# Value products on array quarters, a two-piece mask, transposed statistics, half of the query norms inside the exponential, and re-ordered queues

## The reference

```python
qkv = x @ Wqkv;  q, k, v = split(qkv)                  # 128 -> 3 * 1024
q = l2norm(q) * qs;  k = l2norm(k) * ksc               # norm over each head's 64 numbers
q = q * cos * scale + rotate_half(q) * sin * scale     # and k with 1 / scale
sim = q . k * 8 (own window and the one before);  masked;  attn = softmax(sim);  out = attn @ v
x = x + out @ Wo
xn = (x - mean) / sqrt(var + 1e-5) * g + b
x = x + (a * gelu(gate)) @ W2,   a, gate = split(xn @ W1 + b1)
```

## Time and profile before

| what | value |
|---|---|
| median of 3 runs | 3455.47 us (3453.51 to 3456.21) |
| the profiled execution's own time | 3455.64 us |
| its span, first to last instruction | 3453.9 us |
| PE busy (matmul) | 3233.1 us, 94% |
| DVE busy | 3171.4 us, 92% |
| POOL busy | 2706.3 us, 78% |
| ACT busy | 2438.2 us, 71% |
| mean granted clock of PE | 0.978 of full |

### The profile page before, as it was taken

How to read it: one execution, slowest core, us unless ns; L and a number is a source line. 1 busy time by engine, 2 the same in 40 slices (tenths; PEclk the granted TensorE clock), 3 DMA queues, 4 the chain that set the end, 5 groups by cost and what they waited for, 6 DMA issues and landing times.

```text
span 3453.9 us, 108159 instructions
## 1 busy us (share of the span) xinstructions
PE 3233.1 (94%) x45916; PEld 2089.8 (61%) x46108; DVE 3171.4 (92%) x2914; ACT 2438.2 (71%) x3945; POOL 2706.3 (78%) x1265
## 2 busy tenths in 40 slices
PE   5657999999999999999999999999999999999996
PEld 3325666666666666666666666666666666666663
DVE  6759999999999999999999999999999999999992
ACT  4645777777777777777777777777777777777764
POOL 4547888888888888888878888888888888888871
PEclk9889999999999999999999999999999999999996
DMA  2001111122111122111122111112211122211111
GB/s 77 2 0 32 40 42 39 40 55 57 38 44 39 39 53 57 41 42 42 38 52 54 47 39 41 42 51 52 50 39 40 42 52 51 49 41 39 41 41 39
DMA packets 150433, 148.32 MB, mean 43 GB/s; under 512 B 39228, under 2 KB 95424, under 8 KB 149952
## 3 DMA queue, kind: packets, MB, share of 16 engines
q1 hardware_dynamic: 149952, 141.39, 16.6%
HBM read 19.62 MB, written 2.10 MB: 6 GB/s over the span
## 4 chain that ended last, share of the span: by engine, by line
PE 38%; DVE 26%; ACT 12%; issue 10%; POOL 5%; SPq 2%; DMA 1%; ACTq 0%; DVEq 0%; POOLq 0%
PE bank L574 11%; PE bank L673 7%; DVE rot L1405 6%; PE mid L583 4%; DVE rot L1411 4%; DVE raw L1397 4%; PE mid L624 4%; PE bank L644 4%; DVE Pr L1369 4%; PE mid L611 4%; ACT sq L911 3%; POOL FX L1164 3%; ACT mid L944 3%; DVE mx L1347 2%; ACT raw L903 2%
## 5 line engine op out<-in xcount | busy, mean ns | idle before, releaser
L574 PE MATMUL bank<-wqkv,xs 128*128 128x512 f32 x2304 | 1133.0, 605 | 11.0 <-ACT raw L903 8.5
L1145 POOL TENSOR_TENSOR rr<-ssm,nhalf 128x32 f32<-128x32 f32 x192 | 1051.8, 5478 | 16.0
L1155 POOL TENSOR_TENSOR swp<-raw,TS 128x1024 f32<-128x1024 f32 x384 | 896.8, 2356 | 175.1 <-DVE raw L1397 175.1
L903 ACT ACTIVATE raw<-bank 128x512 f32<-128x512 f32 x768 | 447.5, 598 | 424.2 <-PE bank L574 258.4
L574 PEld LDWEIGHTS bank<-wqkv,xs 128*128 128x128 f32 x2304 | 394.4, 191 | 310.4 <-issue 267.2
L1397 DVE TENSOR_TENSOR raw<-raw,rr 128x2048 f32<-128x2048 f32 x192 | 489.9, 2552 | 16.8 <-POOL rr L1145 16.8
L1391 DVE TENSOR_REDUCE ss<-sq 128x16 f32<-128x1024 f32 x384 | 463.5, 1207 | 23.7 <-ACT sq L911 12.1
L583 PE MATMUL mid<-ident,rot 128*128 128x128 f32 x3072 | 416.6, 279 | 52.0 <-DVE rot L1411 23.1
L583 PEld LDWEIGHTS mid<-ident,rot 128*128 128x128 f32 x3072 | 336.9, 142 | 204.1 <-ACT OT L950 134.6
L1411 DVE TENSOR_TENSOR rot<-rot,swp 128x2048 f32<-128x2048 f32 x192 | 440.1, 2292 | 21.1 <-DVE rot L1405 1.4
L1405 DVE TENSOR_TENSOR rot<-raw,TC 128x2048 f32<-128x2048 f32 x192 | 434.1, 2261 | 0.0
(11 more groups left out here) (134 smaller groups left out, 4443.8 us busy)
## 6 DMA issues: line engine op xcount, KB each, us to landing
PT<-PTd SPq DMA_DIRECT2D x1344, 64.0 KB
xs<-F SPq DMA_DIRECT2D x192, 64.0 KB, 1.9
wqkv<-d_wqkv SPq DMA_DIRECT2D x36, 256.0 KB, 3.3
VT<-V SPq DMA_DIRECT2D x144, 64.0 KB
BT<-PTd SPq DMA_DIRECT2D x288, 32.0 KB
fwo<-d_fwo SPq DMA_DIRECT2D x6, 512.0 KB, 4.1
d_out<-X SPq DMA_DIRECT2D x8, 256.0 KB, 2.3
w<-d_w SPq DMA_DIRECT2D x6, 341.0 KB
```

The costliest lines, as they stand in the source:

```text
L574: nc.tensor.matmul(bank[bk][:, :], xs[:, j, :], wqkv[:, c, :], start=True, stop=True)\
L903: nc.scalar.activation(raw[:, j % 2, c * 512:(c + 1) * 512], bank[RAW_BANK[c]][:, :], ACT.Copy)\
L1145: pool.tensor_tensor(rr[:, :], ssm[:, :], nhalf[:, :], ALU.pow).then_inc(rr_ready, 1)
L1155: last = pool.tensor_tensor(dst[:, :, :, t, :], src[:, :, :, 1 - t, :], tab.unsqueeze(2).broadcast_to([P, 2, HEADS, 32]), ALU.mult)
```

## The change

- **Value products.** `pv` becomes `pv_first` and `pv_second`. Each head's product of 128 keys by 128 queries is cut into one of the lower 64 keys by 96 queries and one of the upper 64 keys by 64 queries, on quarters of the array; the products with the keys in front come first and now use 64 rows. `pv_second` waits for the end of `pv_first` (`pv_half`), for which `to_v` and one DMA of `bands` now wait too.
- **Mask.** The identity product over 128 rows becomes one product over 64 rows for each bank, in different halves of the array.
- **Statistics.** `centred` becomes four plain transposes; the mean is taken off in `ffn_normed` by a bias, for which POOL makes two more small tensors in `ffn_rstd`.
- **Norm inside the exponential.** Eight of the sixteen query heads are not multiplied by their norm on DVE. Their scale and bias go into the exponential: eight ACTIVATEs of 128 x 64 with a scale and a bias read per row, then one of 128 x 512 for the other eight heads. DVE gets `max_bias` (128 x 8); `normed` shrinks from 2048 to 1536 numbers a row, `less_max` from 1024 to 512.
- **Orders.** As below, in every kind of slot. `ffn_stats` moves from second in DVE's slot of kind 0 to last in that of kind 3.

```diff
-            def pv(n, b, j):
+            def low_keys(j, u, h, start):
+                hc = (2 * u + h) * DH
+                return nc.tensor.matmul(OUT_BANK[u // 4][h * DH:(h + 1) * DH, (u % 4) * P:(u % 4) * P + 3 * W],
+                                        V[0:DH, j % 2, hc:hc + DH], PT[0:DH, 0:3, h * HH + u, :],
+                                        start=start, stop=True, skip_group_check=True)
...
+            def pv_first(n, b, j):
...
+                for u in range(4):
+                    for h in range(2):
+                        high_keys(j, 4 + u, h, j == 0 and u == 0)
+                        mm = low_keys(j, u, h, j == 0 and u == 0)
+                mm.then_inc(pv_half, 1)
+
+            def pv_second(n, b, j):
+
+                pe.wait_ge(pv_half, n + 1)
+                for u in range(4):
+                    for h in range(2):
+                        high_keys(j, u, h, False)
+                        mm = low_keys(j, 4 + u, h, False)
                 mm.then_inc(pv_done, 1)
```

```diff
-                    nc.tensor.matmul(bank[3 + h][:, :], identb[:, :],
-                                     maskb[:, 1 if j == 0 else 0, :, :].rearrange("p h k -> p (h k)"),
+                    r = slice(h * DH, (h + 1) * DH)
+                    nc.tensor.matmul(bank[3 + h][:, :], pickb[r, :],
+                                     maskb[r, 1 if j == 0 else 0, :, :].rearrange("p h k -> p (h k)"),
...
-                    mm = nc.tensor.matmul(bank[7][:, t * P:(t + 1) * P], FX[:, t * P:(t + 1) * P], cen[:, :],
-                                          start=True, stop=True)
+                    mm = nc.tensor.transpose(bank[7][:, t * P:(t + 1) * P], FX[:, t * P:(t + 1) * P], ident[:, :])
...
             def exps(n, b, j):
+                act.wait_ge(bias_ready, n + 1)
                 act.wait_ge(sub_ready, n + 1)
-                nc.scalar.activation(mid[:, 1:3, :], mid[:, 1:3, :], ACT.Exp).then_inc(exp_ready, 1)
+                for h in range(2):
+                    for u in range(4):
+                        x = mid[:, 1 + h, u * DH:(u + 1) * DH]
+                        hd = 2 * u + h
+                        nc.scalar.activation(x, x, ACT.Exp, scale=rr[:, j, hd:hd + 1], bias=mb[:, h, u:u + 1])
+                x = mid[:, 1:3, 4 * DH:8 * DH]
+                nc.scalar.activation(x, x, ACT.Exp).then_inc(exp_ready, 1)
...
-                pool.tensor_tensor(rstd[:, :], vpe[:, :], nhalf[:, 0:TPB], ALU.pow).then_inc(rstd_ready, 1)
+                pool.tensor_scalar(nmean[:, :], mv[:, :, 0], -1.0, None, ALU.mult).then_inc(mean_ready, 1)
+                pool.tensor_tensor(rstd[:, :], vpe[:, :], nhalf[:, 0:TPB], ALU.pow).then_inc(rpow_ready, 1)
+                pool.wait_ge(rpow_ready, b + 1)
+                pool.wait_ge(mean_ready, b + 1)
+                pool.tensor_tensor(nmr[:, :], rstd[:, :], nmean[:, :], ALU.mult).then_inc(rstd_ready, 1)
```

Before, the attention steps were in this order: `proj 1, proj 0, scores, qk_back 3, 0, proj 3, 2, pv, proj 4, 5, qk_back 1, 2, out_proj`, with `ffn_out` ahead of `out_proj` in kind 2. ACT's and DVE's:

```diff
 # ACT, kind 0 (tail)
-                    step(c, 0, squares, 1)
                     step(c, 4, o_to_sbuf)
+                    step(c, 0, squares, 1)
                     step(c, 3, to_v, 4)
                     batch(c, 2, ffn_normed)
-                    batch(c, 2, ffn_affine)
                     step(c, 3, to_v, 5)
                     step(c, 2, qk_to_sbuf, 1)
+                    batch(c, 2, ffn_affine)
+                    batch(c, 2, lin_to_sbuf, 0)
                     step(c, 2, qk_to_sbuf, 2)
-                    batch(c, 2, lin_to_sbuf, 1)
 # ACT, kind 2
-                    step(c, 0, to_raw, 1, True)
+                    step(c, 0, to_raw, 0, True)
+                    step(c, 0, to_raw, 1, False)
                     batch(c, 2, gelu, 1)
                     batch(c, 2, gelu, 2)
-                    step(c, 0, to_raw, 0, False)
                     step(c, 0, squares, 0)
                     step(c, 2, qk_to_sbuf, 3)
                     step(c, 2, qk_to_sbuf, 0)
-                    step(c, 0, to_raw, 3, False)
-                    batch(c, 2, lin_to_sbuf, 2)
                     step(c, 3, exps)
                     step(c, 0, to_raw, 2, False)
+                    step(c, 0, to_raw, 3, False)
+                    step(c, 4, o_to_sbuf)
+                    batch(c, 2, lin_to_sbuf, 2)
                     step(c, 0, squares, 1)
-                    step(c, 4, o_to_sbuf)
 # DVE, every kind
                     step(c, 0, sumsq, 0)
-                    batch(c, 2, ffn_stats)
                     step(c, 3, sums)
                     step(c, 3, sums_inverse)
+                    step(c, 3, probs)
                     step(c, 0, sumsq, 1)
-                    step(c, 3, probs)
                     step(c, 3, probs_back)
                     step(c, 1, cos_part)
                     step(c, 1, rotated)
+                    step(c, 2, maxes)
+                    step(c, 2, max_bias)
+                    step(c, 2, less_max)
                     step(c, 0, normed)
-                    step(c, 2, maxes)
-                    step(c, 2, less_max)
```

More of the change, by code:

```diff
@@ L260, in adaln_block @@
         pv_done = sem("pv_done")
+        pv_half = sem("pv_half")
         oT_out = sem("oT_out")
@@ L725, in slot @@
+                    batch(c, 2, ffn_in, 1, 0, False, 7)
                     after(c, (4, prob_ready))
                     step(c, 3, scores)
+                    after(c, (3, qkT_out[2]), (5, oT_out), (3, qkT_out[0]))
+                    step(c, 2, qk_back, 0, True)
                     after(c, (3, qkT_out[1]), (5, oT_out), (3, qkT_out[3]))
-                    step(c, 2, qk_back, 3, True)
-                    after(c, (3, qkT_out[2]), (5, oT_out), (3, qkT_out[0]))
-                    step(c, 2, qk_back, 0, False)
@@ L731, in slot @@
[L731 to L734 removed]
+                    step(c, 2, qk_back, 3, False)
+                    after(c, (0, raw_out[1]), (4, v_out[1]), (1, raw_out[2]))
+                    step(c, 0, proj, 2, False, 0)
+                    after(c, (0, raw_out[0]), (4, v_out[0]), (1, raw_out[3]))
@@ L735, in slot @@
+                    step(c, 0, proj, 3, False, 1)
+                    after_batch(c, (2, lin_out[1]), (2, lin_out[0]), (2, nT_out), (2, xn_ready), (3, yo_ready), (3, lin_out[2]), (3, ge_ready[2]), (3, ge_ready[1]), (3, ge_ready[0]))
+                    batch(c, 2, ffn_in, 0, 1, False, 7)
                     after(c, (2, qkT_out[0]), (3, qkT_out[2]), (5, oT_out))
                     after(c, (2, qkT_out[3]), (3, qkT_out[1]), (5, oT_out))
-                    step(c, 4, pv)
-                    after(c, (0, raw_out[3]), (0, raw_out[1]), (4, v_out[0]))
@@ L765, in slot @@
-                    step(c, 0, proj, 3, False, 0)
-                    after_batch(c, (2, ge_ready[2]), (2, ge_ready[1]), (2, ge_ready[0]), (2, lin_out[0]), (2, lin_out[1]), (2, nT_out), (2, xn_ready), (3, yo_ready), (3, lin_out[2]))
+                    step(c, 2, qk_back, 3, False)
+                    after(c, (0, raw_out[1]), (4, v_out[1]), (1, raw_out[2]))
+                    step(c, 0, proj, 2, False, 0)
+                    after(c, (0, raw_out[0]), (4, v_out[0]), (1, raw_out[3]))
+                    step(c, 0, proj, 3, False, 1)
@@ L782, in slot @@
-                    batch(c, 2, ffn_out, 7)
-                    step(c, 4, out_proj)
                 else:
-                    after(c, (4, v_out[0]), (1, raw_out[3]), (1, raw_out[1]))
+                    after(c, (4, v_out[1]), (1, raw_out[2]), (1, raw_out[1]))
                     step(c, 0, proj, 1, True, 0)
-                    after(c, (4, v_out[1]), (1, raw_out[2]), (1, raw_out[0]))
+                    after(c, (4, v_out[0]), (1, raw_out[3]), (1, raw_out[0]))
                     step(c, 0, proj, 0, False, 1)
@@ L1474, in slot @@
                     step(c, 1, rotated)
+                    step(c, 2, maxes)
+                    step(c, 2, max_bias)
+                    step(c, 2, less_max)
                     step(c, 0, normed)
-                    step(c, 2, maxes)
-                    step(c, 2, less_max)
-            slots(8, slot)
+                    batch(c, 1, ffn_stats)
+            slots(4, slot)
             for b in range(B - 2, B):
```

273 lines of the change are left out of this document (145 added, 128 removed).

## The result

The changed kernel takes **3752.79 us** (median of four runs, 3748.69 to 3763.28) against 3455.84 us (3453.51 to 3456.82) before on the same chip: a ratio of 1.086, 95% interval 1.085 to 1.0876. It is slower by 297 us. The forecast was 3720 us, slower, with a range that holds the result.

What follows compares the result with a forecast made beforehand. Before, DVE was taken to set the pace in kinds 0, 1 and 3, an ACT and PE chain in kind 2. Changed, a loop of waits: 26.1 + 20.8 + 16.6 + 7.4 = 70.9 us a batch; 3455.6 + 264 = 3720 us, range 3480 to 3840.

Steps and rivals of the forecast that it cites:

- the walk: The changed queues followed once round a batch, as a loop where everything waits: 70.9 us a batch, where it was 65.17.
- C3 to E1: From the end of kind 3's `cos_part` on DVE to the end of kind 1's exponential on ACT: 26.1 us.
- E1 to E2: From the end of kind 1's exponential to the end of kind 2's: 20.8 us, 17.7 before.
- E2 to E3: From the end of kind 2's exponential to the end of kind 3's: 16.6 us.
- E3 to C3: From the end of kind 3's exponential to the end of DVE's `cos_part` of kind 3: 7.4 us.
- What the forecast listed: Signs: `maxes` idle over 100 us for scores, `to_raw` waiting for `proj 0`, `ffn_in` for gelus, table to exponential some 15 us.
- PE's small terms: PE's gains: value products 0.3 to 0.5 us a slot, mask 0.2 or nothing, `centred` 0.5 a batch; mostly worth nothing.
- The shares: Signs of being right: busy near 84% of a batch on DVE, 85% on PE, 80% on ACT.
- the price of the exponential: On ACT, pieces 0.30 us apart make the exponential 3.0 us for 1.0; ends 2.25 and 3.85; three on the loop.
- What the orders do: The step walking the changed queues of all engines round a batch; its four parts sum to 70.9 us, 3720 us in all.
- the shorter DVE and PE work buys nothing: Everything on the loop waits for something, so the work saved on DVE and PE gains no time.
- Rival (a): Faster: the loop has unseen slack and the feed-forward steps hide, 60.9 us a batch, 3260 us; chance 0.15.

Runs made afterwards that it cites:

- one exponential (3): The changed kernel with one exponential over all heads and the full `normed` and `less_max` on DVE: 3783.51 us.
- orders alone (1): The kernel before with only the new orders, its own arithmetic kept: 3749.37 us.
- Experiment 4: The changed kernel with `proj 1` copied ahead of the gelus and `proj 0` behind (kind 2), and `qk_back 2` ahead of `out_proj` (kind 1), put back: 3617.76 us.
- Experiment 8: The kernel before, in its own orders, with the new quarters, mask and plain transposes on PE, but one exponential and full norm on DVE: 3459.27 us.
- 11: The kernel before with one move: `normed` behind `maxes` and `less_max` in every kind: 3709.52 us.
- 12: The kernel before with all the new orders but one: `normed` stays ahead of `maxes` and `less_max`: 3706.34 us.
- experiment 6: Experiment 4 plus POOL's `ffn_rstd` ahead of `sin_part` in kind 3, four heads normed in the exponential, linear copy 2 behind the second `squares`: 3597.59 us.

## Why the prediction came out right, and where its reasons did not hold

Eight kernels differ in only three things. Their medians in us:

| DVE's `normed` | other orders | arithmetic of before | changed arithmetic |
|---|---|---|---|
| ahead | before | 3457 (before) | 4126 |
| last | before | 3710 | 3754 |
| ahead | new | 3706 | 4121 |
| last | new | 3749 | 3753 (changed) |

**The mechanism held for the changed kernel.** The four links of the walk, from the end of `cos_part` of kind 3 over the ends of the three exponentials and back, beside what the traces have (us, medians over the batches):

| link | walk | changed | one exponential (3) | orders alone (1) | before |
|---|---|---|---|---|---|
| C3 to E1 | 26.1 | 25.9 | 25.5 | 24.7 | 24.4 |
| E1 to E2 | 20.8 | 21.0 | 20.6 | 20.9 | 17.7 |
| E2 to E3 | 16.6 | 16.7 | 15.7 | 16.1 | 15.5 |
| E3 to C3 | 7.4 | 7.6 | 9.9 | 9.8 | 7.4 |
| sum | 70.9 | 71.2 | 71.7 | 71.5 | 65.0 |

Every link of the changed kernel is met within 0.2 us, so the number is no luck of errors that cancel. The forecast is 33 us short because the mean period is 71.50 and not 70.9 (28 us) and 5 us lie outside the 46 periods. What the forecast listed is there: `maxes` waits 357.9 us (over 100), `to_raw` in kind 2 waits 2.07 us for `proj 0`, `ffn_in` waits 168.8 us for the gelus, and from the gelu's table load to the end of the next exponential are 15.0 us (1736.76 to 1751.75). Experiment 4 shortens the second link alone and gains what was expected. Experiment 8 bears out that less work on PE alone would have bought nothing in the kernel before.

**The exponential was sized right.** Eight pieces take 2.44 us in kind 2, and one 0.397:

```profile
L985 ACT ACTIVATE mid<-mid,mb,rr 128x64 f32<-128x64 f32 x1536 | 470.1, 397 | 1.7
```

(2.44 - 0.397) / 7 = 0.292 us from start to start, forecast 0.30. By the Trainium skill's figures (ScalarE: Activation LUTs, What ACT_TABLE_LOAD costs) the estimate was 0.33; the trace decides for 0.292.

**PE's small terms.** With the keys in front the value products last 2.26 us (1729.21 to the start of `proj 5` at 1731.47) for 2.49 before, a gain of 0.2 where 0.3 to 0.5 was taken. The mask's two products are followed by the scores 0.3 us after their start, where it was 0.5 us before: the 0.2 that the text allowed. `centred` went from 1.13 to 0.60 us, as taken. The Trainium skill's rule on draining at a change of the tiling mode (TensorEngine Tiling (Array Packing), Key Properties) was to speak for the slower side. Whether TensorE drains between mask and scores no row can tell; here the scores follow sooner than before.

```profile
1723.88 0.39 PE L614 MATMUL mid<-maskb,pickb 64*128 64x512 bf16 x2
1724.20 1.48 PE L621 MATMUL mid<-kT,qT 64*32 64x64 f32 x128
```

**The shares.** DVE was to be near 84% of a batch and is 81% in the window, PE 85% and is 86%, ACT 80% and is 76%. DVE's slow runs of `normed` beside POOL vanished (mean 1.747 us). One reading of the lines was a little high, without weight for the sum: `ffn_stats` makes the slot of kind 0 longer by 0.9 us before (from `cos_part` at 1714.86 to 1731.24 are 16.38 us, for 15.47), not by 1.17.

**What was wrong.** First, the price of the exponential. The prediction puts three exponentials on the loop at their full length, 3 x 2.0 us more in a batch that becomes 5.7 us longer, and takes the ends of its range from that price. In the table one exponential, 1.9 us shorter, takes 0.4, 0.4 and 1.0 us off the three links that hold it (the longer `less_max` and `normed` that go with it included), and the fourth grows by 2.3. Beside the path that was walked lies another, over PE's value products to `o_to_sbuf`, that is nearly as long, and POOL's power beside `cos_part` is a third. So the walk gives the time of the kernel that was walked, and not what one of its terms is worth: by it the kernel with the orders alone was to take 3590 us, and it takes 3749. That both arithmetics end within 4 us of each other in the new orders is a coincidence, as far as the links show: they differ.

Second, the step "What the orders do" lays the loss on the steps of ACT and PE. Experiments 1, 11 and 12 show that this is half of it: DVE's move alone costs 253 us and the rest alone 249, but both together 292. Either makes the scores late, and the second finds most of its loss taken already; this reason is argued from the waits, not shown by a run of its own. That the shorter DVE and PE work buys nothing is right for this combination (3749 and 3753). Nor would the old orders have kept a gain of the arithmetic: with the changed arithmetic and the old orders it is 4126 us. That `normed` last is *needed* by the split exponential, and is worth 372 and 368 us there, was not seen. The traces show two reasons. With `normed` last, DVE has work for the length of the exponential (`normed` and `sumsq`, 1.75 + 1.2 = 2.95 us, for 2.93). And `max_bias` no longer meets `sin_part`.

**Rival (a)**, 3260 us, asked for a loop that hides. No run reached it. In the best of the kernels with a split exponential, experiment 6, DVE still waits 103.9 us for the scores and 160.3 us for a power of POOL that met `rotated`.

Still open: how the 372 us divide between `max_bias`, the missing cover and the granted clock. No kernel took one of them away alone. And no order was found that beats the kernel before.

## What to carry to other kernels

When a step is moved behind one that waits for another engine, list what it delays (here `sumsq`, which frees the buffer of the squares) and who stands behind that: work that filled a wait, moved behind it, can keep the wait alive. The costs of moves on one loop don't add; run each alone and all together before a cause gets its price. A walk round the loop gives the time of that kernel, but a term of it is worth its length only as long as no other path is nearly as long. Work taken off the engine that sets the pace is worth its length only if what pays for it doesn't lengthen the chain through the other engines.
